# A fused decoder layer on one core: keys and values projected one step ahead, and another order of GpSimd's work

## What is computed

```
c = exp(-exp(lmlg)) * exp(1j*theta)
conv[n] = sum_m c**(n-m) * x[m] + last_conv * c**(n+1)       # over the 32 sequence steps
x1 = layernorm(x + real(conv) * x)
q, k, v = relu(x1@Wq+bq), relu(ctx@Wk+bk), relu(ctx@Wv+bv)   # 16 heads of 16 channels
o = softmax(q k^T / 4) v + q                                 # per item n, over its 256 rows
x2 = layernorm(x1 + ln_g * norm(o) + ln_b)
xn = rmsnorm(x2) * scale; e = argmin distance(xn, centroids) # 8 experts
out = layernorm(x2 + expert_e(xn) + x2)                      # a * silu(g), then down
```

## Time and profile before

| | us |
|---|---|
| median of 3 runs | 1263.86 |
| lowest, highest | 1254.69, 1266.94 |
| the profiled execution | 1257.0 |
| its span in the trace | 1255.2 |
| mean granted TensorE clock | 0.935 of full speed |

### The profile page before, as it was taken

The page is one execution under the profiler, slowest core; times in us unless marked ns, Lnnn a source line. Parts: engine busy times, 40 slices in busy tenths (PEclk is TensorE's granted clock), DMA queues, the critical chain, the costliest instruction groups (busy, mean ns, idle before and its releaser), DMA issues.

```text
span 1255.2 us, 27516 instructions
## 1 busy us (share of the span) xinstructions
PE 1119.9 (89%) x8060; PEld 820.0 (65%) x8061; DVE 942.7 (75%) x2416; ACT 669.9 (53%) x1416; POOL 783.9 (62%) x932
## 2 busy tenths in 40 slices
PE   3799989999999998989999999752999999999996
PEld 2466666666666666656666666431888888888885
DVE  7558998988988998999898898763555555555553
ACT  4166776766667776767676777641222222222221
POOL 4637888888878988879888865561233333333333
PEclk9689999999989999999999999555999999999998
DMA  4676676665555565556556555042111111111110
GB/s 131 146 179 194 174 207 183 182 156 139 141 140 146 149 158 137 147 139 161 136 146 156 136 134 126 11 151 59 44 51 47 43 50 50 49 47 48 50 51 22
DMA packets 90826, 144.91 MB, mean 115 GB/s; under 512 B 12663, under 2 KB 78336, under 8 KB 84513
## 3 DMA queue, kind: packets, MB, share of 16 engines
q1 hardware_dynamic: 83616, 126.09, 38.6%
q0 software_dynamic: 6528, 16.99, 4.6%
q10 hardware_dynamic: 576, 0.53, 0.2%
HBM read 91.44 MB, written 53.03 MB: 115 GB/s over the span
## 4 chain that ended last, share of the span: by engine, by line
PE 45%; DVE 19%; POOL 15%; issue 10%; DMA 8%; SPq 2%; ACT 1%; POOLq 0%; DVEq 0%; ACTq 0%
PE Y L454 10%; PE G L422 8%; PE A L422 8%; DVE neg_max_sb L1243 7%; PE S L1004 3%; PE M L988 3%; DMA k_st<-k_pieces 3%; DMA k_pieces<-k_lo 3%; DVE oq L1370 3%; POOL buckets L802 2%; PE GT L432 2%; PE O L980 2%; POOL rs L729 2%; POOL by_re L694 2%; PE M L960 2%
## 5 line engine op out<-in xcount | busy, mean ns | idle before, releaser
L1243 DVE TENSOR_REDUCE neg_max_sb<-S 128x2 f32<-128x512 f32 x512 | 328.3, 682 | 71.0 <-PE S L1004 69.2
L864 ACT ACTIVATE probs<-T 128x512 f32<-128x512 f32 x512 | 277.9, 595 | 148.1 <-PE T L1017 136.8
L1004 PE MATMUL S<-k_st,q_st 48*128 48x256 f32 x1024 | 215.3, 321 | 46.3 <-DMA k_st<-k_pieces 27.8
L1004 PEld LDWEIGHTS S<-k_st,q_st 48*128 48x128 f32 x1024 | 147.3, 194 | 123.7 <-issue 53.5
L1017 PE MATMUL T<-q_st,k_st 49*128 49x256 f32 x1024 | 211.9, 321 | 9.8 <-ACT probs L864 8.1
L1017 PEld LDWEIGHTS T<-q_st,k_st 49*128 49x128 f32 x1024 | 148.0, 195 | 28.3 <-ACT probs L864 17.0
L399 ACT ACTIVATE gT<-GT 128x512 f32<-128x512 f32 x71 | 42.5, 599 | 209.4 <-PE GT L432 209.4
L980 PE MATMUL O<-probs,v_aug 128*32 128x256 f32 x2048 | 151.0, 416 | 0.7 <-ACT probs L864 0.7
L378 POOL DMA_INDIRECT out<-res,token x71 | 76.4, 1077 | 103.3 <-DVE res L499 98.8
L454 PE MATMUL Y<-dn_sb,gT 128*128 x568 | 134.2, 379 | 0.8 <-ACT gT L399 0.8
L802 POOL DMA_INDIRECT buckets<-row,slot x64 | 69.7, 1089 | 85.0 <-DVE slot L1425 74.8
(11 more groups left out here) (184 smaller groups left out, 2541.1 us busy)
## 6 DMA issues: line engine op xcount, KB each, us to landing
q_st<-q_pieces SPq DMA_DIRECT2D x64, 256.0 KB
k_st<-k_pieces SPq DMA_DIRECT2D x64, 256.0 KB
xr<-buckets SPq DMA_DIRECT2D x71, 129.0 KB, 2.1
xt<-in_x SPq DMA_DIRECT2D x32, 256.0 KB, 6.3
ct<-in_ctx SPq DMA_DIRECT2D x32, 256.0 KB, 6.8
q_pieces<-q_hi SPq DMA_DIRECT2D x32, 256.0 KB, 2.1
q_pieces<-q_lo SPq DMA_DIRECT2D x32, 256.0 KB, 2.2
q_st<-q_pieces SPq DMA_DIRECT2D x64, 128.0 KB
```

The lines of the kernel that those rows point to most:

```text
L864: a_.activation(probs[:, h % 8].rearrange("p k t -> p (k t)"), T_ps[h % 2][:, :], ACT.Exp, scale=DH ** -0.5).then_inc(s["exp_ok"], 1)
L1004: last = t_.matmul(S_ps[h % 2][:, c * TOK:(c + 1) * TOK], q_st[base:base + STACK, h, c * P:(c + 1) * P], k_st[base:base + STACK, h, :], st ...
L1243: v.tensor_reduce(neg_max[:, cur.mod(2), :, h], S_ps[h % 2][:, :].rearrange("p (c t) -> p c t", c=NTC), AX.X, ALU.max, negate=True).then_i ...
```

## The change

Keys and values of an item are projected one step earlier: in step t the engines handle those of `kv = t+2`, at the same head positions, and the queries stay at t+1. The first context is loaded twice ahead, and in steps -2 and -1 a few pieces stand at other places (context flips and copies at h 0 and h 4, the values of item 0 in step -1). In SyncE's list the key pieces of t+2 follow the read of q's half 0, and k half 0 of t+1 is read between the two writes of q's pieces. In GpSimd's list the scatter of an item moves to the next step, behind `weigh`; the double product of the next item moves from the head of the step to behind `conv_input`, ahead of the root rs2 and `rms`.

```diff
@@ SyncE
+                def write_keys(item):
+                    if active(item):
+                        wait(sp, "k_ok", item, 4, 2)
+                    write_piece(item, k_dram, 0, k_hi, k_out)
+                    if active(item):
+                        wait(sp, "k_cut", item)
+                    write_piece(item, k_dram, 1, k_lo, k_out)
...
                 def step(t):
-                    nxt = t + 1
+                    nxt, kv = t + 1, t + 2
                     load_x(t + 3)
-                    load_context(t + 3)
+                    load_context(t + 4)
                     write_neg(t - 1, 1)
                     read_neg(t - 1, 1)
+                    if t.k == -2:
+                        write_keys(kv)
...
                     write_piece(nxt, q_dram, 0, q_hi, q_out)
+                    read_k(nxt, 0)
                     if active(nxt):
                         wait(sp, "q_cut", nxt)
                     write_piece(nxt, q_dram, 1, q_lo, q_out)
                     read_q(nxt, 0)
-                    if active(nxt):
-                        wait(sp, "k_ok", nxt, 4, 2)
-                    write_piece(nxt, k_dram, 0, k_hi, k_out)
-                    if active(nxt):
-                        wait(sp, "k_cut", nxt)
-                    write_piece(nxt, k_dram, 1, k_lo, k_out)
+                    if t.k > -2:
+                        write_keys(kv)
                     write_neg(t, 0)
-                    read_k(nxt, 0)
                     read_neg(t, 0)
                     read_q(nxt, 1)
                     read_k(nxt, 1)
@@ GpSimd
+                def scatter(item):
+
+                    if not active(item):
+                        return
+                    p = item.mod(2)
+                    wait(pool, "slot_ok", item, SLOT)
+                    wait(pool, "id_ok", item)
+                    wait(pool, "rms", item, 4)
+                    for c in range(NTC):
+                        g.indirect_dma_start(out=buckets[:, :], out_offset=bass.IndirectOffsetOnAxis(ap=slot[:, p, c:c + 1], axis=0),
+                                             in_=row[:, p, c, :], in_offset=None, bounds_check=PAD - 1,
+                                             oob_is_err=False).then_inc(scat[p], 16)
...
-                    conv_products(t + 3)
                     weigh(b)
+                    if b.k - 1 < SEQ - 3:
+                        scatter(b - 1)
+                    if t.k == -2:
+                        conv_products(t + 3)
...
-                    if n.k > 0:
-                        cut(n, k32[:, :, :], k_hi, k_lo, "k_ok", "k_cut", k_out)
+                    if n.k + 1 > 0:
+                        cut(n + 1, k32[:, :, :], k_hi, k_lo, "k_ok", "k_cut", k_out)
                     conv_imag(t + 3, 1)
                     rstd(a, "lnx", 4, mvx, rsx, "rstdx")
-                    if active(b):
...
                     conv_input(t + 3)
+                    conv_products(t + 4)
                     rstd(a, "ln2", 4, mv2, rs2, "rstd2")
                     rms(a)
+                    if b.k >= SEQ - 3:
+                        scatter(b)
@@ TensorE (ScalarE's copies move in the same way)
-                        if h in (6, 7) and active(n):
-                            wait(pe, "ctT_ok", n)
+                        if h == 4 and t.k == -1:
+                            for half in range(NTC):
+                                values(kv - 1, half)
+                            wait(pe, "q_ok", n, 4)
+                            flip_context(kv)
+                        if h in (6, 7) and active(kv):
+                            wait(pe, "ctT_ok", kv)
...
+                        if h in (11, 12) and t.k != -2:
+                            values(kv, h - 11)
...
+                        if h == 15 and t.k != -2:
+                            flip_context(kv + 1)
```

More of the change, by code:

```diff
@@ L872, in step @@
                             exponentials(prv, h + 1)
+                        if h == 0 and t.k == -2:
+                            copy_context(kv)
                         if h == 0:
@@ L881, in step @@
                             a_.activation(qn[:, n.mod(4)].rearrange("p c d -> p (c d)"), M_ps[2][:, :], ACT.Copy).then_inc(s["qn_ok"], 1)
[L882 to L885, removed]
+                        if h == 15 and t.k != -2:
+                            copy_context(kv + 1)
+                        if h == 4 and t.k == -1:
+                            copy_values(kv - 1)
+                            copy_context(kv)
                         if h == 1 and active(prv):
@@ L901, in step @@
                                                       bias=bq_sb[:, c:c + 1]).then_inc(s["q_ok"], 1)
[L902 to L905, removed]
+                        if h == 7 and active(kv):
+                            wait(act, "k_pe", kv, 2)
+                            wait(act, "k_cut", kv - 1)
+                            wait_ring(act, k_out[(kv - 1).mod(2)], kv - 1, 2, 32)
                             for dst in (k_hi, k32):
@@ L913, in step @@
                             a_.activation(xnT[:, :, :].rearrange("p o t -> p (o t)"), M_ps[2][:, :], ACT.Copy).then_inc(s["xnT_ok"], 1)
[L914 to L918, removed]
+                        if h == 13 and t.k != -2:
+                            copy_values(kv)
                         if h == 4 and active(b):
@@ L990, in project, with values, flip_context @@
                     return last
+                def values(item, c):
+                    if not active(item):
+                        return
+                    wait(pe, "k_ok", item, 4)
+                    if (item - 2).edge():
+                        wait(pe, "o_ok", item - 4, 4, 2)
+                    if c == 0:
+                        if item.k == 0:
+                            pe.wait_ge(s["setup_dve"], BIAS)
+                        t_.matmul(M_ps[1][:, :], ones_bf[:, :], bv_cut[:, :], start=True, stop=False)
+                    for ic in range(NCH):
+                        last = t_.matmul(M_ps[1][:, c * C:(c + 1) * C], ctT[:, ic, c * P:(c + 1) * P], wv_sb[:, ic, :],
+                                         start=False, stop=(c == NTC - 1 and ic == NCH - 1))
+                    last.then_inc(s["v_pe"], 1)
+                def flip_context(item):
+                    if not active(item):
+                        return
+                    wait_ring(pe, ctx_in_s[item.mod(2)], item, 2, 16)
+                    wait(pe, "neg_ok", item - 3, 2, 1)
+                    if (item - 3).edge():
+                        wait(pe, "q_ok", item - 2, 4)
+                        wait(pe, "o_ok", item - 5, 4)
+                    flip(M_ps[0], ct[:, item.mod(2)]).then_inc(s["ctT_pe"], 1)
                 def scores(cur, h):
@@ L1037, in step @@
                                 weighted_sum(a, 3)
-                        if h == 2 and n.k == 0:
+                        if h == 2 and kv.k == 0:
                             pe.wait_ge(s["params"], PARAMS * 16)
@@ L1333, in step @@
                             bias_pieces()
+                        if h == 15 and t.k == -2:
+                            first_key_cut()
                         if h == 1 and t.k == -1:
```

40 lines of the change are left out of this document (25 added, 15 removed).

## The result

The changed kernel took 1370.36 us (median of 4 runs, 1364.44 to 1372.02), the kernel before 1265.4 beside it: ratio 1.0839, interval 1.0767 to 1.0910. It is slower, as forecast, but by 105 us and not by 46, and it lies above my range. The profiled execution has a span of 1367.3 us against 1255.2.

The account below looks back on a forecast made before the run. No engine plainly full; VectorE ends last where keys come in time. Steps of 16.0 + 7.2 + 2.6 = 25.8 us against 23.88 add 49 us over 26 steps, less 1: median 1310, own range 1290 to 1325, over cases 1240 to 1352.

Parts of the forecast that it names:

- Keys and values ahead: TensorE's stalls on the key stack go: 0.76 us a step at most, little where the double product meets `u`.
- The start: Queries and keys of item 0 exchange places in one chain: between 0 and 2 us, taken as 0.
- The double product ahead of the root: Behind the root rsx, conv_input and double product hold VectorE's gains and y2: 2.6 us a step taken.
- from X to T: Quiet half, attention norm's moments end (X) to last layer norm's moments end (T): from 7.2 to near 9.8 us.
- rival 3: Full exclusion holds VectorE and idle TensorE's clock falls: step 27.4 us, 1348 us in all; chance 0.19.
- From T to X: First half, last layer norm's moments to attention norm's: 16.0 us against 16.7, since `u` is mostly freed.
- T to X over 17: Sign of being wrong: a first half over 17 us would mean that it kept its holds.
- The sum: New step 16.0 + 7.2 + 2.6 = 25.8 us against 23.88, for 26 steps; median 1310 us.
- its 3.4: Holding in the quiet half by the skill page's rule alone, issue order deciding: 3.4 us a step.
- the row's 2.2: Holding in the quiet half by onehot_bf's 188 ns median, passing though k_lo was first: 2.2 us a step.
- The scatter's move: GpSimd's first half gains two scatters (2.4 us), loses the double product (2.37), so reaches rsx about as before.

Follow-up runs that it names:

- kv_only: The changed kernel with the whole of GpSimd's old order, only keys and values one step ahead: 1244.73 us, ratio 0.9891; five more rounds 1244.31 us, 0.9903.
- two_waits: The changed kernel plus two GpSimd waits: conv_input waits for both gains, the double product for both x1 instructions; 113 us faster than the changed kernel.
- two_waits_product: two_waits plus a second, useless double product right behind conv_input in steps 2 to 27: 1346.79 us.
- filler_6: The changed kernel plus 6 useless matmuls in TensorE's idle time ahead of head 0, steps 2 to 27: 1319.42 us.
- kv_scatter: kv_only with the scatter moved to the next step, the double product at the head of the step: 1327.94 us.

## Why the prediction was wrong

- **Keys and values ahead: right.** Worth "little" where the double product meets `u`; measured 12 to 17 us, 0.55 us a step in kv_only, within my 0.76 at most. No DMA wait of the old size took the stall's place (in kv_only TensorE waits 2.0 us in all for the maxima, and for no other DMA).
- **The start: wrong.** I compared only the chain of q and k and took 0 to 2 us. The queue in between held it: the query's write stands behind a context load that waits for TensorE. In the changed kernel the first maximum is 5.9 us later, the first X 8.3; where the last 2.4 come from stays open.
- **The double product ahead of the root: right in kind and, in part by luck, in size.** Forecast 9.8 us from X to T, measured 9.98. The terms behind it were others: I had conv_input hold the gains in every step (1.05 us) and the double product hold y2 for 1.2. In 14 steps the gains passed, the cast was held for 0.5 us and y2 for 2.1; in 10 steps the first gain was held for 1.0 and the product of place and one-hot for 2.1, which is the order that I had left to rival 3. two_waits and two_waits_product show that it is this hold.
- **From T to X: this step failed.** I put it at 16.0 us "against 16.7 today", counting on freed holds; it is 17.85. The failed term is the clock, which my sum put at nothing. I had written the mechanism down as rival 3 (TensorE idle for about 3 us, then a slower clock) and given it 0.19, although the key stalls had shown the same with 2 us of idle time, and my own sum made TensorE idle for just as long in every step. In none of the 24 steps is the granted clock from T to X above 0.92. filler_6 prices it at up to 1.7 us a step and brings T to X to 16.18, close to my 16.0. `u` was also held after all (2.27 us at the median, where I expected 0.7 to 1.0), but T to X hardly needs it: 17.57 with `u` free (two_waits_product). So my sign "T to X over 17" came true, but not by the holds I had read into it.
- **The sum.** (17.85 - 16.0) x 26 = 48, (9.98 - 9.8) x 26 = 5 and the start's 8 make 61 us: 1310 + 61 = 1371, against 1370 measured; that it fits to 1 us is luck, since the medians of before alone differ by that much. Of the rivals, 3 had 27.4 us a step against 27.8 measured, by two errors that nearly cancel: 0.7 too much holding (3.5 against 2.8) and 1.15 too little from T to X (16.7 against 17.85). It was right on the clock and wrong in tying it to the full hold: the clock fell at least as far in the steps where both gains passed (0.84 from T to X at the mean, against 0.87 in the others).
- **The page of the Trainium skill** named in the prediction (SBUF — State Buffer, section "Who interferes with whom") has issue order decide. The hold of 2.8 us lies between its 3.4 and the row's 2.2, but not because the order failed: by the starts of the rows, every gain, every product of place and one-hot and every y2 of the changed kernel that was held came behind the GpSimd operation that held it, and y2's first instruction, which passed, started 0.14 us ahead. Where the rows don't agree is `u`, held by a bias whose row starts 0.35 us behind its own, and the one-hot of before. The same section says that an instruction with two SBUF inputs contends only with GpSimd work that reads SBUF; y2 beside memsets (0.98 us) and beside the double product (3.01) agrees.
- **The scatter's move.** I costed it as room on GpSimd, neutral. That was right only together with the double product's: alone it makes the offset late (kv_scatter, up to 2.28 us).

## What to carry to other kernels

Before work of GpSimd is moved, list VectorE's instructions at its new place by their operands: beside a long operation that reads SBUF, two-input SBUF instructions wait for its end here (y2's second took 2.61 us instead of 0.47), a cast does too (0.64 instead of 0.16), and reductions from PSUM don't (0.68 us each). An idle GpSimd may be what keeps VectorE fast; two waits gave back 113 us here. And a stall put on TensorE's feeder is not over with its own length: where TensorE goes idle for some 3 us each step, add the clock to the price, since 2.8 us of holding became 3.9 us of step.

## What the runs showed of the hardware that I had not expected

- Six useless matmuls a step, some 2.7 us of work for TensorE (half of the 5.35 us of twelve), made the kernel 51 us faster (granted clock 0.87 to 0.98 over the steady stretch).
- GpSimd memsets, which read nothing, stretched VectorE's small cast from 0.16 to 1.08 us and the scale-and-shift x1 from 0.73 to 1.29 us, while the two-input y2 beside them kept 0.98.
- The start of a row does not always say who goes first. In the kernel before, the one-hot, issued right behind oq while k_lo's row had begun some 0.45 us earlier, passed in 17 of 25 steps and was held in 8. In the changed kernel `u` was held in 18 of 24 steps by a bias whose row starts 0.35 to 0.6 us behind its own. y2's second instruction, issued 0.25 us behind the double product, was held each time (14 of 14).
